# One loop over the images, a float8 cast on another engine, and half of a turned copy made by a transfer

## The reference, cut to what matters

```
x  = x + vss(group_norm(x))          # layer 0
     # vss: layer norm -> in_proj 96 -> 192+192 -> depthwise 3x3 conv + SiLU -> u (192 x 4096)
     #      selective scan of u in 4 directions: by rows, by columns, and both reversed
     #      h = exp(delta*A)*h + delta*u*B ; y = sum_n C*h     (16 states for each channel)
     #      layer norm, gate, out_proj, skip; layer norm, 3x3 conv, GELU, 3x3 conv, channel attention
t  = tokens(x)                        # 4096 tokens of 96
t  = t + linear_attention(layer_norm(t))
t  = t + ffn(layer_norm(t))
     # ffn: h = relu(q_acc(q_acc(q_mul(t) @ q_mul(W1)) + q_mul(b1)))     96 -> 384
     #      y = q_acc(q_acc(q_mul(h) @ q_mul(W2)) + q_mul(b2))           384 -> 96
     # q_mul rounds to float8 e5m2, q_acc rounds to float16
```

## Time and profile before

| | us |
|---|---|
| three runs, median | 13487.59 (13481.8 to 13489.0) |
| the profiled execution: its own time | 13489.0 |
| the profiled execution: span of the trace | 13487.2 |
| busy: PE / DVE / ACT / POOL | 10625.8 / 11940.9 / 6836.5 / 10380.0 |
| granted TensorE clock, mean | 0.897 of full |

### The profile page before, as it was taken

How to read it: one execution, slowest core, us unless ns; L and a number is a source line. 1 busy time by engine, 2 the same in 40 slices (tenths; PEclk the granted TensorE clock), 3 DMA queues, 4 the chain that set the end, 5 groups by cost and what they waited for, 6 DMA issues and landing times. The chain is left out here.

```text
span 13487.2 us, 94856 instructions
## 1 busy us (share of the span) xinstructions
PE 10625.8 (79%) x24646; PEld 4153.7 (31%) x24646; DVE 11940.9 (89%) x8647; ACT 6836.5 (51%) x10172; POOL 10380.0 (77%) x4597
## 2 busy tenths in 40 slices
PE   6777887778887788877878778777787777888777
PEld 2333322333233332333323333233332323323333
DVE  7999779996799968999689996899968999689996
ACT  4545455554545545555455554554545545555454
POOL 4999459994599945999459994699936999369993
PEclk9899889998899988899989998899988999888998
DMA  4676446764467744677446774577735777357773
GB/s 139 215 219 216 113 129 216 219 214 111 135 214 220 214 106 138 214 220 216 102 143 216 220 214 96 148 215 220 213 94 151 214 220 213 92 154 215 217 216 88
DMA packets 734722, 2403.55 MB, mean 178 GB/s; under 512 B 173200, under 2 KB 175248, under 8 KB 722768
## 3 DMA queue, kind: packets, MB, share of 16 engines
q1 hardware_dynamic: 734192, 2397.58, 61.2%
HBM read 2300.18 MB, written 67.11 MB: 176 GB/s over the span
## 5 line engine op out<-in xcount | busy, mean ns | idle before, releaser
L1253 POOL TENSOR_TENSOR state<-state,c_sb 128x1024 f32<-128x1024 f32 x3072 | 7179.9, 2357 | 472.3 <-ACT carry L1080 470.1
L1009 PE MATMUL ps<-state,wt 128*128 128x512 f32 x12288 | 6346.1, 659 | 160.2 <-ACT ya L1073 107.1
L1009 PEld LDWEIGHTS ps<-state,wt 128*128 128x128 f32 x12288 | 2558.6, 212 | 3059.5 <-issue 2479.9
L1212 DVE TENSOR_TENSOR_SCAN state<-decay,carry,ps 128x1024 f32<-128x1024 f32 x1440 | 3379.3, 2347 | 107.5 <-DVE ps L1199 38.7
L1080 ACT COPY carry<-state 128x1 f32<-128x1 f32 x3072 | 585.9, 191 | 4861.0 <-DVE state L1212 4852.0
L986 PE MATMUL ps<-parts,sel 114*128 114x512 bf16 (+1 forms) x3840 | 1290.0, 421 | 2089.5 <-DVE state L1212 2087.3
L1242 POOL TENSOR_TENSOR dbu<-b_sb,du 128x1024 f32<-128x1024 f32 x1152 | 2716.7, 2358 | 230.7 <-DVE du L1227 230.7
L1199 DVE TENSOR_TENSOR ps<-ps,du 128x1024 f32<-128x1024 f32 x1920 | 2322.3, 1210 | 2.4 <-PE ps L986 1.4
L1122 ACT ACTIVATE decay<-delta,a_neg 128x1024 f32<-128x1024 f32 x1920 | 2195.4, 1144 | 6.8
L1212 DVE TENSOR_TENSOR_SCAN state<-ps,carry,dbu 128x1024 f32<-128x1024 f32 x864 | 2013.2, 2330 | 4.2 <-POOL dbu L1242 3.5
L986 PEld LDWEIGHTS ps<-parts,sel 114*128 114x128 bf16 (+1 forms) x3840 | 260.2, 100 | 3639.4 <-DVE state L1212 3364.8
(11 more groups left out here) (217 smaller groups left out, 10257.9 us busy)
## 6 DMA issues: line engine op xcount, KB each, us to landing
c_sb<-bc SPq DMA_DIRECT2D x2048, 512.0 KB, 4.5
c_sb<-bc SPq DMA_DIRECT2D x2048, 256.0 KB, 5.6
b_sb<-bc SPq DMA_DIRECT2D x768, 512.0 KB, 4.7
b_sb<-bc SPq DMA_DIRECT2D x768, 256.0 KB, 5.5
x_nat<-x SPq DMA_DIRECT2D x17, 1536.0 KB, 14.5
gates<-gate_a SPq DMA_DIRECT2D x8, 2048.0 KB, 6.8
x_tok<-x SPq DMA_DIRECT2D x288, 48.0 KB, 1.8
gn<-gn_t SPq DMA_DIRECT2D x8, 1536.0 KB, 7.1
```

The lines of the kernel that those rows point to most:

```text
L1009: mm = pe.matmul(py[:, q * CH:(q + 1) * CH], col("ident"), state[:, slot(g, n), q * CH:(q + 1) * CH], start=(n == 0), stop=False)
L1212: dve.tensor_tensor_scan(state[:, slot(g, n), way], rate, what, 0.0 if fresh else carry[:, n:n + 1], ALU.mult, ALU.add)\
L1253: pool.tensor_tensor(state[:, slot(g, n), :], state[:, slot(g, n), :], c_sb[:, n % CRING, :], ALU.mult).then_inc(S["weighted"], 1)
```

## The change

Three things change. First, the loop over the images becomes one hardware loop, `with nc.Fori(0, NB) as b`, whose body stands in the program once; the addresses of x and of the output are computed from its counter. Second, `ur_out` turns both halves in one pass over 128 partitions into `ur_cols`, which grows to 128 partitions, and a further copy puts the lower half in its place in `ur`; `ur_in` is now waited for at 64. Third, the cast to float8 moves from POOL to ACT, as `quantise` at lag 6 of the feed-forward part.

```diff
-    ur_cols = at("ur_cols", [DR, W, HH], F32, 3 * KB16 + HALF)
+    ur_cols = at("ur_cols", [128, W, HH], F32, 3 * KB16 + HALF)
...
-            sp.dma_start(x_nat[:, :], xv[b]).then_inc(nat_in, 16)
+            sp.dma_start(x_nat[:, :], xv[bass.ds(b, 1)].rearrange("a c l -> (a c) l")).then_inc(nat_in, 16)
...
-                    sp.dma_start(half_of[:, :, 0:HH], ur_cols[:, :, :]).then_inc(S["ur_in"], 16)
+                    sp.dma_start(half_of[:, :, 0:HH], ur_cols[0:DR, :, :]).then_inc(S["ur_in"], 16)
+                    sp.dma_start(half_of[:, :, HH:H], ur_cols[DR:128, :, :]).then_inc(S["ur_in"], 16)
...
-                    pool.wait_ge(S["ur_in"], 48)
+                    pool.wait_ge(S["ur_in"], 64)
...
-                            pe.wait_ge(S["ur_in"], 48)
+                            pe.wait_ge(S["ur_in"], 64)
...
-                        act.activation(turned, rc(src[0:DR, :]), ACT.Silu, bias=bias[0:DR, :])
-                        here = ur[DR:128, :].rearrange("p (w h) -> p h w", h=H)[:, HH + first:HH + first + count, :]
-                        return act.activation(here, rc(src[DR:128, :]), ACT.Silu, bias=bias[DR:128, :])
+                        return act.activation(turned, rc(src), ACT.Silu, bias=bias)
...
-                    following = (b + 1) % NB
+                    following = sp.snap((b + 1) % NB)
...
+                    def quantise(j):
+                        act.wait_ge(S["h_biased"], j + 1)
+                        if j >= 2:
+                            act.wait_ge(S["y_mm"], j - 1)
+                        act.activation(h8[:, j % 2, :, :], h16b[:, j % 2, :, :], ACT.Copy, saturate=False)\
+                           .then_inc(S["h_quant"], 1)
...
-                              (5, half), (7, y_half))
+                              (5, half), (6, quantise), (7, y_half))
...
-                    for j in range(NCH):
-                        pool.wait_ge(S["h_biased"], j + 1)
-                        if j >= 2:
-                            pool.wait_ge(S["y_mm"], j - 1)
-                        pool.tensor_copy(h8[:, j % 2, :, :], h16b[:, j % 2, :, :], saturate=False)\
-                            .then_inc(S["h_quant"], 1)
...
-        for b in range(NB):
-            def img(ap, b=b):
-                return ap[b]
+        with nc.Fori(0, NB) as b:
+            def img(ap):
+                return ap[bass.ds(b, 1)].rearrange("a c l -> (a c) l")
```

## The result

Four runs of the changed kernel have a median of 13596.42 us (13584.24 to 13603.49), four of the kernel before beside them 13484.69 us (13481.26 to 13489.0). The ratio is 1.0082, 95% interval 1.0064 to 1.0099: slower by 111.7 us, where 121 had been forecast over the profiled execution and 13609 us as the time. The profiled execution after took 13593.77 us, its granted clock was 0.894 of full (0.897 before).

The account below looks back on a forecast made before the run. Bound: stages ending in all-engine barriers, with ACT's list setting the feed-forward step. Cast 72 + copy 28 + jump 21 = 121 us over the profiled 13489.0 gives 13610, stated as 13609 us; range 13560 to 13685.

Parts of the forecast that it names:

- The bound: Whole kernel: each part ends in an all-engine barrier, so its gain or loss reaches the end whole, eight times.
- The cast on ACT: Feed-forward part: ACT's list sets the step, a cast takes 1.55 us; 9.0 us an image, 72 in all, bounds 48 to 87.
- The rival that the cast hides: Feed-forward part: a round trip, not ACT's list, sets the step; 0 in place of 72 us, 13537 us; chance 0.08.
- The pass that goes: `ur_out` in `prep_b`: two ACT passes, 4.1 us an image, go, but ACT then waits for DVE's taps; counted 0.
- The copy: `prep_b`: second copy of 4096 runs delays both `ur_rows` copies; 3.5 us an image, 28 in all, bounds 21 and 79.
- dry gap: `prep_b`, second copy: transfer engines run nearly dry about 0.7 us before the next data; 0.9 us counted an image.
- Rival 1: `prep_b` copy: writing out 4096 runs takes 9.88 us by itself; 79 in place of 28 us, 13660 us; chance 0.15.
- Rival 3: `prep_b`: second copy free or nearly so; 8 to 0 in place of 28 us, 13589 to 13581 us; chance 0.07.
- The jump: Between images: each jump back costs one load of instructions, 3 us; seven make 21 us, bounds 1 and 41.
- Rival 4: Between images: several stalls for every engine, 8 us or more a jump; 56 in place of 21, 13644 us; chance 0.07.
- The computed addresses: Loop counter and addresses on SP: some register operations beside its waits, with no cost counted.
- Rival 5: Scan: one resident body is fetched better than eight, giving back DVE idle time; 13462 us at half of it; chance 0.03.

Follow-up runs that it names:

- e2_cast: Only the float8 cast moved from POOL to ACT, on the kernel before, images written out: 13516.02 us, ratio 1.0026.
- e6_ur_first_copy: Kernel before with copies to `ur` issued ahead of the gates' stores, plus the single 128-partition turning pass and second copy: 13452.18 us, ratio 0.9978.
- e12_cast_twice: Kernel before with the cast on ACT, each cast done twice, the first into a spare tile nobody reads: 13639.03 us, ratio 1.0112.
- e3_copy: Only the single turning pass over 128 partitions and the second copy, on the kernel before: 13515.0 us, ratio 1.0021.
- e4_cast_copy: Changed kernel without the hardware loop: cast and copy edits on the kernel before, images written out: 13543.82 us, ratio 1.0047.
- e11_warm_all: Changed kernel plus unread products filling TensorE's last two waits in `prep_a`: 13568.63 us, ratio 1.0061.
- e8_warm: Kernel before plus three unread products filling TensorE's waits ahead of the last two input projections of `prep_a`: 13458.55 us, ratio 0.9981.
- e5_ur_first: Kernel before with SP issuing the three copies to `ur` ahead of the gates' stores instead of behind: 13423.83 us, ratio 0.9956.
- e7_loop_pair: Kernel before with a hardware loop of four turns over a body of two images, so three jumps back: 13478.23 us, ratio 0.9996.
- e1_loop: Only the hardware loop over images, one image in its body, on the kernel before: 13507.08 us, ratio 1.0021.

## Why the prediction was right, step by step

**The bound.** That each stage ends in a barrier and so passes its gain or loss on eight times held: the stage differences add up to the difference of the spans within 0.2 us.

**The cast on ACT: mechanism right, 9.0 us an image forecast, 7.6 measured.** The cast was sized too large. Its 1.55 us came from 1.04 ns a column, of f32 passes; it took 1.38 us of the list, 0.90 ns a column. Six full steps make 8.3 in place of 9.3, and with -0.6 + 0.3 for the edges 8.0. The last 0.4 us are within what was chosen for the edges. (In the changed kernel `post` holds the cast and the loop's 0.5 us an image; its 60.7 us are no larger than e2_cast's 61.0, since images of `post` differ by 3.3 us with the clock's course, see e6_ur_first_copy.) The rival that the cast hides fell by the rows (no idle time, and e12_cast_twice).

**The pass that goes: 0, confirmed** by the 1.98 us that ACT waits for DVE behind it.

**The copy: size right, 3.5 us an image forecast, but not as its two terms had it.** Between kernels in which `prep_a` ended on the same clock it is 3.4 (e3_copy less before), 3.7 (e4_cast_copy less e2_cast) and 3.5 (e11_warm_all less e8_warm). In the profiled execution after it is 2.85 in the mean: four images take 87.3 to 87.8 us, four 86.0 to 86.4, and these four spend 10.2 us of `prep_b` at half clock where the others spend 13.4 to 13.8. The forecast had 2.6 us for moving the runs at 205 GB/s and 0.9 for a dry gap, with full transfer engines. The second copy moved at 141 GB/s in e6_ur_first_copy with the engines at a share of 0.79, so that 0.52 MB take 3.7 us; no separate gap is needed. That 2.6 + 0.9 comes near it is luck. What paces the second copy, the writing out of its runs or something else, is open. Rival 1 (9.9 us to write the runs out) fell by the issue of 3.8 us in e3_copy and 2.92 in e5_ur_first: most of the 9.88 us were the gates. Rival 3 fell by e3_copy's 3.4 us an image.

The prediction read the rule of the Trainium skill (DMA: Bandwidth & Descriptors, section Why small descriptors are slow (HBM only)) against the wrong row. It set the runs' 205 GB/s against the 524 GB/s of the gates, but the gates go to DRAM. Inside SBUF the `ur_rows` copies with rows of 8 KB move at 262 GB/s, and the first copy of runs at 202: small pieces cost a fifth there, not 60%. That agrees with what the same section says of a remote transfer with 128-byte packets, that it "still hits 78% of max link BW". By 262 GB/s the rule's sum would have been 2.0 us and not 1.0, and 3.4 to 3.7 were measured; the 141 GB/s of the second copy the rule does not give.

**The jump: 3 us forecast, 3.3 to 4.0 measured.** The seven images behind a jump take 57.5 us in `prep_a` in e11_warm_all, those of e8_warm 54.2: 3.3 in the mean. The clock's course is not the same in all of them: where it rose 14.5 to 14.9 us behind the start they take 56.2 to 56.8, where it rose at 21.6 they take 58.9 or 59.0. In e7_loop_pair two jumps cost 3.9 and 4.0, and the third image, with 7.7, had a fall of the clock besides. The forecast of POOL's first clear, 3 us behind the barrier, was too low: it came 4.1 to 5.3 us behind. In that trace TensorE's first product came 4.4 us behind the barrier in the mean of the seven, and their `prep_a` grew by 3.7 (60.5 against 56.9, with a fall of the clock in each, as before). Rival 4 (8 us or more at each jump) fell: in the profiled execution after, TensorE, ACT, POOL and SP began at most 6.0 us behind the barrier, and no `prep_a` of any trace grew by 8. The sentence of the Trainium skill (Runtime: NRT & Kernel Launch, section Instruction fetch mechanics) that a branch breaks the prefetch agrees with the trace: 7 transfers of instructions lie in the 5.2 us between the branch and the first instruction. The prediction's one load for an engine fits 6 or 7 for all five; which of them belongs to which engine does not show. By the 45 ns of the small loop the term would have been nil. The computed addresses on SP, which the prediction put beside SP's waits and so at nothing, cost 0.5 us an image, 4 us in all (e1_loop).

**Rival 5** fell: the scan is 1300.46 us after and 1300.80 before.

**The sum.** 72 + 28 + 21 = 121 was forecast; the stages show 60.7 + 22.8 + 23.7 - 2.7 = 104.5 in the profiled executions, and the medians 111.7. What was forecast as seen in the profile came, but for POOL's clear: the step 5.06 (5.2 forecast), the last `ur_rows` copy 3.8 us later (3 to 4), the period 1693.0 (1694.5). That the sum is this near is partly luck: 3 us an image in `prep_a`, and 3 to 5 in `post`, hang on where the clock falls, which no step of the prediction had. In e2_cast it hid 23 of 61 us.

**What stays open.** What puts the clock on one course or the other in `post`, 235.0 or 238.3 us an image and more, and with it 17.5 us of e6_ur_first_copy. And what holds the second copy of runs to 141 GB/s.

## What to carry to other kernels

Moving work from an idle engine to one whose list sets the step costs its full length in each step, however short the new instruction: look for the engine without an idle time in the step, not for the one with the smaller share of the page. On a queue of transfers, put what someone waits for first; here that was worth 60 us, as much as the cast on ACT cost. And look at what stands behind a transfer on its queue: in e6_ur_first_copy a copy that nobody waited for held up stores that somebody did. When parts of a change are timed alone, compare the stages and not only the totals, since TensorE's clock can give or take some us in a stage that nobody touched.

## What the runs showed of the hardware

- The granted clock before the last projections of `prep_a` stood at 1.00 or at 0.50 of full behind a wait of the same length (1.86 and 1.87 us). In the images written out one behind the other, it stayed up where it had risen 15.0 to 15.4 us behind the start of the stage and fell where it had risen at 15.5 to 18.1 us; that moved 3 us of a 57 us stage. With products without use in the wait it stayed up in all 32 images of four kernels; that was worth 25 of 13484 us.
- With the same instructions (the kernel before) `post` took 235.0, 238.3 or 240.1 us, with 52.7, 59.2 or 62.6 us of it at half clock.
- Behind a jump back over a body of about 3,000 products TensorE, ACT, POOL and SP began 3.6 to 6.0 us behind the barrier in the changed kernel, with 6 or 7 transfers of instructions ahead of the first of them, the branch itself being 45 ns.
- 4096 runs of 128 bytes inside SBUF moved at 202 GB/s, a second such copy right behind them at 141, rows of 8 KB inside SBUF at 262. They hold up the next transfer's issue for 2.9 to 3.8 us, and for 9.9 us behind 3 MB of other stores.
- A cast of 1536 columns from float16 to float8 takes 1.48 us on ACT (1.38 to the next start), and took 1.86 or 1.47 on POOL.
